# Where the relu rows of eight half-width steps are kept, and when VectorE sums them

## The chip, the core and the metric

The kernel runs on one core of a Trainium2 chip. The metric is the device time of one execution in microseconds, the median over runs. Below, PE is TensorE, DVE VectorE, ACT ScalarE, POOL GpSimd and SP SyncE; a transfer is issued from the queue of SP, ACT or POOL.

## The reference, cut to what matters

```python
e = stack([tbl_f[ids[:, f]] for f in range(32)], axis=1)      # 512 x 32 x 16, gathered rows
xk = x0 = e
for W in (W0, W1, W2):                                        # 64 outputs each
    xk = relu(einsum('bmd,bhd,mhk->bkd', x0, xk, W))
    outs.append(sum(xk, axis=2))                              # the sums that the change moves
h = concatenate([concatenate(outs, axis=1), dense_ctx], axis=1)   # 512 x 208
h = maximum(h @ W_top1 + b_top1, 0)
h = maximum(h @ W_top2 + b_top2, 0)
y = h @ W_top3                                                # 512 x 1
```

## The kernel before, in words

**Tiling.** The batch of 512 is cut into ten blocks: blocks 0 to 3 are half-width (32 examples each, 512 columns of example times dimension), blocks 4 to 9 are full-width (64 examples, 1024 columns). A step is a pair (layer, block), so there are 30 steps. A step of layer 1 or 2 multiplies 128-partition tiles of the fields with tiles of the hidden values elementwise, and PE contracts the products with the weights into a PSUM accumulator `acc`. Most products are made by DVE (line 746), in units of one to three tiles, into the buffer `vz`, which has nine places that are filled in turn; some are made by POOL (line 691) into `pz`, four places. For the five layer-0 steps of blocks 0 to 4, ACT makes the products as squares (line 810).

**Order.** The order of the steps is written out by hand (`BEGUN`, line 71), and planner functions make one program for each engine from it. `ORDER` (line 291) is the steps by the place of their last contraction: (0,0), (0,1), (1,0), (0,2), (1,1), (2,0), (0,3), (1,2), (0,4), (2,1), (1,3), and so on to (2,8), (2,9). PE's program is one list, in which a product of DVE or of POOL, once its turn has come, holds all that stands behind it.

**After the contraction of a step.** ACT writes the relu of `acc` into `relu_out` (line 858), a ring of RRING = 3 places that the steps take by their place in `ORDER`. From there the rows go three ways: by DMAs from ACT's queue into `hidden` (line 869), or through a matmul on PE (line 911, "spread"), as the next layer's factor; and DVE adds up the 16 values of each example (line 756, `dim_sums`) into `feats`. Before a relu takes a place again, ACT waits until the step that had it before is summed, spread and relayed (lines 849 to 856).

**When DVE sums.** `sum_places` (line 342) puts the sum of a step behind the first DVE unit by which at least 6 x 1024 product columns have been made since the step's own last unit, in the order of `ORDER`. `SUMS_AFTER` maps a unit's number to the sums behind it; what is left comes last (`SUMS_LAST`).

**Gathers.** POOL issues 128 indirect gathers (line 674), one for each column of `index`: 48 ahead of its first product, the others between the products as `GATHERS_IN` says. Before the first product of step (1,3) there are 13 more, before its second one more, before its third eight more. Some gathers wait for PE's progress (`PACED`) or for a spread (`BEHIND_SPREAD`). The descriptors of these gathers are written by POOL into a reserved part of each SBUF partition, whose size is an argument of the program's constructor (line 1155).

**The end.** SP copies `feats` of layers 0 and 1 into `stack01` (line 638), each after a count of `sums_done` (line 636). PE's last stage (lines 994 to 1080) needs both, and the sums of layer 2.

The units that matter below are numbered within their step from 0. (1,8) and (1,9) have five DVE units each: three tiles, three, two, two, two. (2,8) begins with a unit of three tiles.

Of the kernel before, what the change touches and what calls it, by code (L numbers as in the profile page):

```python
# [11 lines left out]
P = 128  # L12
BATCH, FIELDS, DIM, HID = 512, 32, 16, 64
CHUNK = 32
N = CHUNK * DIM
# [19 lines left out]
BLOCKS = [(pair, half * N, N, half * GATHERS // 2, GATHERS // 2) for pair in range(NARROW_PAIRS) for half in range(2)]  # L35
BLOCKS += [(pair, 0, PAIR, 0, GATHERS) for pair in range(NARROW_PAIRS, PAIRS)]
LAST = len(BLOCKS) - 1
QUARTERED = max(BLOCKS[b][0] for b in SQUARED) + 1
HALVES = [b for b, block in enumerate(BLOCKS) if block[2] == N]
# [6 lines left out]
def by_field(b):  # L46
    return int(b not in SQUARED)
# [68 lines left out]
PRING = 4  # L116
FRING = 3
RRING = 3
ORING = 2
GRING = 4  # L120
IN_FLIGHT = 3
# [52 lines left out]
def vector_program():  # L174

    program = []
    for step in BEGUN:
        mine = [(step, u) for u in range(len(vector_units(step)))]
        if step in INSIDE:
            at = next(i for i, (outer, u) in enumerate(program)  # L180
                      if outer == BEGUN[BEGUN.index(step) - 1] and u == INSIDE[step])
            program[at:at] = mine
        else:
            program += mine
    return program
# [31 lines left out]
VECTOR = vector_program()  # L217


def vectors_to(step):  # L220

    return max(i for i, (of, _) in enumerate(VECTOR) if of == step) + 1
# [68 lines left out]
ORDER = sorted(BEGUN, key=lambda step: max(i for i, (of, who, u) in enumerate(TENSOR) if of == step and who != "join"))  # L291
# [47 lines left out]
    COLUMNS.append(COLUMNS[-1] + vector_units(_step)[_u][2] * BLOCKS[_step[1]][2])  # L339


def sum_places():

    places, due = {}, list(ORDER)
    for i in range(len(VECTOR)):
        while due and vectors_to(due[0]) <= i + 1 and COLUMNS[i + 1] - COLUMNS[vectors_to(due[0])] >= 6 * PAIR:
            places.setdefault(i, []).append(due.pop(0))
    return places, due


SUMS_AFTER, SUMS_LAST = sum_places()

# [44 lines left out]
def cin_dlrm(nc, table, ids, first_row, unit, pairs, added, parts, w0a, w0b, w0c, w1, w2, wt1, bt1, wt2,  # L399
             bt2, wt3, wt1_dense, dense, out):  # L400
    with ExitStack() as ctx:
        def sb(name, shape, dt=F32):
            return ctx.enter_context(nc.sbuf_tensor(name, shape, dt))
# [4 lines left out]
        def sem(name):  # L408
            return ctx.enter_context(nc.semaphore(name))
# [12 lines left out]
        fields = [sb(f"fields_sb{s}", [P, TILES, PAIR]) for s in range(STREAMS)]  # L422
        hidden = [sb(f"hidden{s}", [P, HHALF, PAIR]) for s in range(STREAMS)]
        relu_out = [sb(f"relu_out{n}", [P, N]) for n in range(RRING)]
        vz = sb("vz", [P, VTILES, PAIR])
        pz = sb("pz", [P, PRING, PAIR])
        oz = [sb(f"oz{n}", [P, PAIR // QUART]) for n in range(ORING)]
        unit_sb = sb("unit_sb", [P, P])
# [48 lines left out]
        relu_done, sums_done = sem("relu_done"), sem("sums_done")  # L477
# [13 lines left out]
        def acc_of(step, ab):  # L491

            return acc[ab * HID:(ab + 1) * HID, ORDER.index(step) % 2, 0:BLOCKS[step[1]][2] // 2]

        def relu_of(step):
            return relu_out[ORDER.index(step) % RRING][:, 0:BLOCKS[step[1]][2] // 2]

        def hidden_of(step, g):
            _, col, cols, _, _ = BLOCKS[step[1]]
            return hidden[stream(step[1])][:, g, col:col + cols]  # L500
# [7 lines left out]
        def quarter_rows(b):  # L508

            pair, _, _, first, rows = BLOCKS[b]  # L510
            return gathered[:, pair % GRING, first:first + rows, :].rearrange("p b d -> p (b d)")
# [16 lines left out]
        def relayed_halves(step):  # L528
            return [1] if step in HALF else range(HHALF)
# [19 lines left out]
        def _(sp):  # L549
# [83 lines left out]
            sp.dma_start(wt2_sb, wt2.rearrange("(m p) n -> p m n", p=P)).then_inc(top_in, 16)  # L633
            half_cols = BATCH // 2
            for layer in range(2):
                sp.wait_ge(sums_done, ORDER.index((layer, LAST)) + 1)
                for ab in range(2):
                    sp.dma_start(stack01[layer * HID:(layer + 1) * HID, ab * half_cols:(ab + 1) * half_cols],
                                 feats[layer][ab * HID:(ab + 1) * HID, :, :].rearrange("p c j -> p (c j)")) \
                      .then_inc(stack01_in, 16)  # L640
# [7 lines left out]
        def _(pool):  # L648
            def rows_landed(i):
                pair, j = divmod(i, GATHERS)  # L650
                b, first = next((b, first) for b, (of, _, _, first, rows) in enumerate(BLOCKS)
                                if of == pair and first <= j < first + rows)
                pool.wait_ge(rows_in[b], 16 * (j - first + 1))
# [60 lines left out]
        def _(dve):  # L714
# [36 lines left out]
            def dim_sums(step):  # L751
                layer, b = step
                pair, col, cols, _, _ = BLOCKS[b]
                first, count = col // DIM // 2, cols // DIM // 2
                dve.wait_ge(relu_done, ORDER.index(step) + 1)
                nc.vector.tensor_reduce(feats[layer][:, pair, first:first + count],  # L756
                                        relu_of(step).rearrange("p (b d) -> p b d", d=DIM),
                                        op=ALU.add, axis=AX_X).then_inc(sums_done, 1)
# [21 lines left out]
        def _(act):  # L780
# [32 lines left out]
            def own_squares(step):  # L813
                b, n = step[1], OWN.index(step)
                _, _, cols, _, rows = BLOCKS[b]
                act.wait_ge(rows_in[b], 16 * rows)
                if n >= ORING:
                    act.wait_ge(oz_used, n - ORING + 1)
                nc.scalar.activation(oz[n % ORING][:, 0:cols // QUART], quarter_rows(b), ACT.Square).then_inc(oz_ready, 1)

# [8 lines left out]
            def contracted(step):  # L829
                act.wait_ge(vz_used, vectors_to(step))  # L830
                if step[0] == 0:
                    act.wait_ge(oz_used, OWN.index(step) + 1)
                if pool_units(step):
                    act.wait_ge(pz_used, pools_used_to(step))
# [8 lines left out]
            def relu(step):  # L843
                n = ORDER.index(step)
                if step in PAIRED:
                    act.wait_ge(joined, JOINED.index(step) + 1)
                else:
                    contracted(step)
                if n >= RRING:
                    layer, b = before = ORDER[n - RRING]  # L850
                    act.wait_ge(sums_done, n - RRING + 1)
                    if (layer + 1, b) in SPREAD or (layer + 1, b) in HALF:
                        act.wait_ge(factor_spread, SPREADS.index(((layer + 1, b), 0)) + 1)
                    if layer < 2 and (layer + 1, b) not in SPREAD:
                        for g in relayed_halves((layer + 1, b)):
                            act.wait_ge(relayed[(layer + 1, b), g], 32)
                half = BLOCKS[step[1]][2] // 2
                nc.scalar.activation(relu_of(step), acc[:, n % 2, 0:half], ACT.Relu).then_inc(relu_done, 1)  # L858

            def relay(step):  # L860
                _, col, cols, _, _ = BLOCKS[step[1]]
                s = stream(step[1])
                act.wait_ge(relu_done, ORDER.index(step) + 1)
                if pools_read((step[0] + 1, step[1])):
                    act.wait_ge(pz_ready, pools_read((step[0] + 1, step[1])))
                for g in relayed_halves((step[0] + 1, step[1])):
                    for ab in range(2):
                        row, at = ab * HID + g * HROWS, col + ab * cols // 2
                        act.dma_start(hidden[s][:, g, at:at + cols // 2],  # L869
                                      relu_of(step)[row:row + HROWS, None, :]  # L870
                                      .broadcast_to([HROWS, MREP, cols // 2])).then_inc(relayed[(step[0] + 1, step[1]), g], 16)
# [3 lines left out]
            for what, step, g in SCALAR:  # L875
                if what == "put":
                    put_factor(step, g)
                elif what == "squares":
                    squares(step, g)
                elif what == "own":  # L880
                    own_squares(step)
                elif what == "copy":
                    copy_hidden(step, g)
                elif what == "fold":
                    fold(step)
                else:
                    relu(step)
                    if step[0] < 2 and (step[0] + 1, step[1]) not in SPREAD:
                        relay(step)
# [12 lines left out]
        def _(pe):  # L902
# [58 lines left out]
            def contract_own(step):  # L961
# [5 lines left out]
                for q in (0, 2, 1, 3):  # L967
                    part = slice(q % 2 * quarter, (q % 2 + 1) * quarter)
                    last = nc.tensor.matmul(acc_of(step, q // 2)[:, part], w0c_sb[:, by_field(b), q, :],  # L969
                                            oz[n % ORING][:, 0:quarter], start=False, stop=q % 2 == 1)  # L970
                last.then_inc(oz_used, 1)
# [191 lines left out]
```

## Time and profile before

| what | value |
|---|---|
| runs | 333.34, 333.96, 334.33 us; median 333.96 |
| profiled execution, its own time | 333.23 us |
| its span in the trace | 331.4 us |
| granted TensorE clock, mean | 0.99 |
| PE, DVE, POOL, ACT busy | 303.6, 267.0, 244.0, 65.3 us |

The span is the stretch between the first and the last recorded instruction. The 1.8 us between it and the execution's own time lie around the program. All stretches below are in microseconds from the start of the span. "Idle before" is the time an engine did nothing before an instruction, and the name behind the arrow is what the profile holds to have ended it.

### The profile page before, as it was taken

The numbers are of one execution on the slowest core, as the hardware profiler recorded it, in microseconds if no ns is written. First come the engines' busy times: TensorE is split into PE (matmuls) and PEld (weight loads), VectorE is DVE, ScalarE is ACT, GpSimd is POOL, SyncE is SP. The second block draws the span as 40 slices with busy tenths as digits, with TensorE's granted clock in tenths as the row PEclk, the third lists the DMA queues.
The fourth block names the chain that finished last, engine by engine and source line by source line (L and its number), as shares of the span: only waits on it lengthen the run. The fifth ranks groups of instructions, "written<-read, shape, count | busy, mean of one in ns | idle before, by whom it ended". The sixth has DMA issues, their size and how long they took to land.

```text
span 331.4 us, 4576 instructions
## 1 busy us (share of the span) xinstructions
PE 303.6 (92%) x1760; PEld 131.7 (40%) x1760; DVE 267.0 (81%) x162; ACT 65.3 (20%) x105; POOL 244.0 (74%) x187
## 2 busy tenths in 40 slices
PE   0469899999869989999999899999999999999996
PEld 0335535654436233333333233344434434434334
DVE  0118399676978999999999999999899999999110
ACT  1030511435000130122122101032213032020011
POOL 5677777778888789999888799999686539966000
PEclk9997999999989999999999999999999999999999
DMA  6364848771388869687679489929979995230000
GB/s 189 95 195 138 242 107 238 206 211 21 87 267 285 292 227 297 230 269 244 203 233 318 141 251 322 323 98 266 385 316 320 313 292 130 60 85 1 0 2 0
DMA packets 32220, 65.43 MB, mean 197 GB/s; under 512 B 5702, under 2 KB 12870, under 8 KB 32198
## 3 DMA queue, kind: packets, MB, share of 16 engines
q1 hardware_dynamic: 20614, 52.28, 46.8%
q10 hardware_dynamic: 7488, 11.80, 12.3%
q0 software_dynamic: 4096, 1.06, 3.9%
q8 instruction: 14, 0.23, 0.3%
q14 instruction: 8, 0.07, 0.1%
HBM read 51.35 MB, written 1.71 MB: 160 GB/s over the span
## 4 chain that ended last, share of the span: by engine, by line
PE 63%; DVE 10%; issue 9%; POOL 4%; ACT 1%; ACTq 0%; DVEq 0%; POOLq 0%
PE acc L956 55%; DVE vz L746 9%; POOL gathered L674 3%; PE factor L1001 2%; PE factor L996 1%; POOL pz L691 1%; PE acc L969 1%; PE factor L911 1%; PE acc L951 1%; PE factor L926 1%; PE factor L1008 1%; DVE feats L756 1%; PE acc L1001 1%; ACT factor L792 0%; ACTq L869 0%
## 5 line engine op out<-in xcount | busy, mean ns | idle before, releaser
L746 DVE TENSOR_TENSOR vz<-fields_sb,factor 128x1024 f32<-128x1024 f32 (+3 forms) x113 | 229.0, 2076 | 32.2 <-PE factor L911 11.1
L956 PE MATMUL acc<-vz,w_sb 128*64 128x512 f32 (+1 forms) x1020 | 197.8, 525 | 6.4 <-DVE vz L746 6.0
L674 POOL DMA_INDIRECT gathered<-in_table,index x128 | 121.8, 952 | 38.1 <-issue 31.0
L691 POOL TENSOR_TENSOR pz<-fields_sb,hidden 128x1024 f32<-128x1024 f32 (+1 forms) x53 | 121.4, 2314 | 19.0 <-DMA hidden<-relu_out 15.0
L956 PEld LDWEIGHTS acc<-vz,w_sb 128*64 128x64 f32 x1020 | 78.6, 139 | 111.3 <-issue 84.1
L956 PE MATMUL acc<-pz,w_sb 128*64 128x512 f32 (+1 forms) x212 | 52.9, 583 | 2.7 <-POOL pz L691 2.7
L858 ACT ACTIVATE relu_out<-acc 128x512 f32<-128x512 f32 (+1 forms) x30 | 15.4, 514 | 111.2 <-PE acc L956 85.8
L792 ACT ACTIVATE factor<-hidden 128x1024 f32<-128x1024 f32 (+1 forms) x26 | 23.6, 914 | 64.5 <-DMA hidden<-relu_out 45.0
L956 PEld LDWEIGHTS acc<-pz,w_sb 128*64 128x64 f32 x212 | 17.1, 137 | 30.1 <-issue 25.7
L746 DVE TENSOR_TENSOR vz<-rotated,factor 128x2048 f32<-128x2048 f32 x10 | 22.4, 2279 | 0.0
L756 DVE TENSOR_REDUCE feats<-relu_out 128x32 f32<-128x512 f32 (+1 forms) x30 | 17.1, 570 | 6.4 <-ACT relu_out L858 6.4
L951 PE MATMUL acc<-vz,w_sb 128*64 128x512 f32 x64 | 16.4, 604 | 0.5 <-DVE vz L746 0.3
L810 ACT ACTIVATE vz<-factor 128x512 f32<-128x512 f32 (+2 forms) x24 | 12.4, 610 | 19.9 <-PE factor L926 14.3
L956 PE MATMUL acc<-vz,w_half 128*64 128x256 f32 (+1 forms) x80 | 13.5, 482 | 2.1 <-ACT vz L810 2.1
L926 PE MATMUL factor<-gathered,added_sb 32*128 32x128 f32 (+1 forms) x160 | 8.7, 344 | 3.6 <-DMA gathered<-in_table,index 3.6
L1018 PE MATMUL acc<-w_half,vz 128*128 128x64 f32 x8 | 1.9, 424 | 9.6 <-ACT w_half L874 9.6
L926 PEld LDWEIGHTS factor<-gathered,added_sb 32*128 32x128 f32 x160 | 6.5, 212 | 6.9 <-issue 6.8
L911 PE MATMUL factor<-relu_out,unit_sb 32*128 32x256 f32 (+1 forms) x56 | 8.7, 499 | 0.6 <-ACT relu_out L858 0.6
L956 PEld LDWEIGHTS acc<-vz,w_half 128*64 128x64 f32 x80 | 5.7, 152 | 8.5 <-issue 4.2
L969 PE MATMUL acc<-oz,w0c_sb 128*64 128x256 f32 (+1 forms) x80 | 9.0, 346 | 0.0
L792 ACT ACTIVATE factor<-own 128x1024 f32<-128x1024 f32 x5 | 5.1, 1027 | 18.7 <-issue 10.3
L951 PEld LDWEIGHTS acc<-vz,w_sb 128*64 128x64 f32 x64 | 4.6, 136 | 10.5 <-DVE vz L746 6.2
(35 smaller groups left out, 52.6 us busy)
## 6 DMA issues: line engine op xcount, KB each, us to landing
fields_sb<-fields SPq DMA_DIRECT2D x48, 512.0 KB, 5.0
rotated<-fields SPq DMA_DIRECT2D x20, 512.0 KB, 6.4
hidden<-relu_out ACTq DMA_DIRECT2D x38, 256.0 KB, 5.7
fields_sb<-fields SPq DMA_DIRECT2D x32, 256.0 KB, 3.3
own<-fields SPq DMA_DIRECT2D x5, 512.0 KB, 5.9
gathered<-in_table,index POOLq DMA_INDIRECT x128, 4.1
hidden<-relu_out ACTq DMA_DIRECT2D x14, 128.0 KB, 3.9
fields<-gathered SPq DMA_DIRECT2D x5, 256.0 KB, 2.2
```

The lines of the kernel that those rows point to most:

```text
L674: nc.gpsimd.indirect_dma_start(gathered[:, pair % GRING, j, :], None, table, bass.IndirectOffsetOnAxis(ap=index[:, i:i + 1], axis=0)).then ...
L691: nc.gpsimd.tensor_tensor(pz[:, at % PRING, 0:cols], fields[s][:, t, col:col + cols], hidden_of(step, g), ALU.mult).then_inc(pz_ready, 1)
L746: nc.vector.tensor_tensor(vz[:, at:at + nt, 0:cols].rearrange("p t (a n) -> p t a n", n=half), src[:, t:t + nt, col:col + cols].rearrange( ...
L756: nc.vector.tensor_reduce(feats[layer][:, pair, first:first + count], relu_of(step).rearrange("p (b d) -> p b d", d=DIM), op=ALU.add, axis ...
L792: nc.scalar.activation(factor_of(step, g), src.rearrange("p (a n) -> p a n", a=2), ACT.Copy).then_inc(factor_put, 1)
L810: last = nc.scalar.activation(made, sums, ACT.Square)
L858: nc.scalar.activation(relu_of(step), acc[:, n % 2, 0:half], ACT.Relu).then_inc(relu_done, 1)
L911: last = nc.tensor.matmul(factor_of(step, g)[:, ab, :], unit_sb[row:row + HROWS, :], relu_of(before)[row:row + HROWS, :], start=True, stop ...
L926: last = nc.tensor.matmul(added_bank(step, t, q), added_sb[row, t, :], rows[row, :], start=True, stop=True)
L951: last = nc.tensor.matmul(acc[side % 2 * HID:(side % 2 + 1) * HID, ORDER.index(step) % 2, 0:cols], weights[:, kt, :], z, start=side < 2, s ...
L956: last = nc.tensor.matmul(acc_of(step, ab), weights[:, kt, :], z[:, ab * half:(ab + 1) * half], start=start and j == 0, stop=stop and j == ...
L969: last = nc.tensor.matmul(acc_of(step, q // 2)[:, part], w0c_sb[:, by_field(b), q, :], oz[n % ORING][:, 0:quarter], start=False, stop=q % ...
```

## The change: places of their own for eight steps

The first eight half-width steps of `ORDER`, which are (0,0), (0,1), (1,0), (0,2), (1,1), (2,0), (0,3) and (1,2), get a relu place each (eight tensors of 512 columns, 2 KB of each partition). The other 22 steps share the ring of three. The sums of the eight no longer stand behind the units of the early steps; one of them stands behind each unit of DVE from unit 0 of (1,8) on, after whatever sum the old rule puts there. That gives: (0,0) behind unit 0 of (1,8), (0,1) behind unit 1, (1,0) behind unit 2, (0,2) behind unit 3, (1,1) behind unit 4; (2,0) behind unit 0 of (1,9), (0,3) behind unit 1, (1,2) behind unit 2. In the kernel before they stood behind unit 5 of (1,0); units 2, 3 and 5 of (1,1); unit 5 of (2,0); units 3 and 5 of (1,2); and unit 1 of (2,1). All other sums stay behind the units that they stood behind. The counts that ACT and SP wait for follow the new order, and the eight relus, with the three first ones of the ring, wait for no sum. The reserved part for gather descriptors becomes 8192 bytes of a partition, half of what it was.

```diff
+KEPT = 8
+KEPT_UNTIL = (1, 8)
...
+KEPT_STEPS = [step for step in ORDER if step[1] in HALVES][:KEPT]
+RINGED = [step for step in ORDER if step not in KEPT_STEPS]
 def sum_places():
-    places, due = {}, list(ORDER)
+    places, due, kept = {}, list(RINGED), list(KEPT_STEPS)
     for i in range(len(VECTOR)):
         while due and vectors_to(due[0]) <= i + 1 and COLUMNS[i + 1] - COLUMNS[vectors_to(due[0])] >= 6 * PAIR:
             places.setdefault(i, []).append(due.pop(0))
+        if kept and i >= VECTOR.index((KEPT_UNTIL, 0)):
+            places.setdefault(i, []).append(kept.pop(0))
+    assert not kept
     return places, due
...
+SUMMED = [step for i in range(len(VECTOR)) for step in SUMS_AFTER.get(i, [])] + SUMS_LAST
...
+        kept = [sb(f"kept{n}", [P, N // 2]) for n in range(KEPT)]
...
         def relu_of(step):
-            return relu_out[ORDER.index(step) % RRING][:, 0:BLOCKS[step[1]][2] // 2]
+            if step in KEPT_STEPS:
+                return kept[KEPT_STEPS.index(step)][:, :]
+            return relu_out[RINGED.index(step) % RRING][:, 0:BLOCKS[step[1]][2] // 2]
...
-                sp.wait_ge(sums_done, ORDER.index((layer, LAST)) + 1)
+                sp.wait_ge(sums_done, max(n for n, step in enumerate(SUMMED) if step[0] == layer) + 1)
...
-                if n >= RRING:
-                    layer, b = before = ORDER[n - RRING]
-                    act.wait_ge(sums_done, n - RRING + 1)
+                if step in RINGED and RINGED.index(step) >= RRING:
+                    layer, b = before = RINGED[RINGED.index(step) - RRING]
+                    act.wait_ge(sums_done, SUMMED.index(before) + 1)
...
-    nc = bacc.Bacc("TRN2", target_bir_lowering=False, num_devices=1)
+    nc = bacc.Bacc("TRN2", target_bir_lowering=False, num_devices=1, dynamic_dma_scratch_size=8192)
```

## Rows read from the trace of the kernel before

**Rows 1.** The page: each engine's busy time, and the chain that ended last.
```profile
PE 303.6 (92%) x1760; PEld 131.7 (40%) x1760; DVE 267.0 (81%) x162; ACT 65.3 (20%) x105; POOL 244.0 (74%) x187
...
PE 63%; DVE 10%; issue 9%; POOL 4%; ACT 1%; ACTq 0%; DVEq 0%; POOLq 0%
```

**Rows 2.** Busy time by stretch: PE, PEld, DVE, ACT, POOL, then clock, DMA share, GB/s.
```profile
250.00:280.00 30.00, 30.00 (x147) 12.40 (x144) 29.57 (x15) 6.93 (x10) 18.49 (x8) 1.00 0.89 273
280.00:314.00 34.00, 34.00 (x164) 13.32 (x160) 27.61 (x14) 4.82 (x6) 21.25 (x10) 1.00 0.15 35
```

**Rows 3.** Timeline of POOL around 95 us: start, length, what, idle before.
```profile
94.54 0.94 POOL L674 DMA_INDIRECT gathered<-in_table,index  x1 [0.30 <-issue]
95.50 1.28 POOL L691 TENSOR_TENSOR pz<-fields_sb,hidden 128x512 f32<-128x512 f32 x1
```

**Rows 4.** All gathers of the kernel: their time, and their time to landing.
```profile
L674 POOL DMA_INDIRECT gathered<-in_table,index x128: 940/944/1114, 3.6 to 218.8; - x128
...
  issue: 31.0, 109
...
DMA to landing us min/median/max: 2.3/4.1/6.4
```

**Rows 5.** Timeline of PE around 95 us.
```profile
96.84 0.87 PE L956 MATMUL acc<-pz,w_sb 128*64 128x256 f32 x4 [2.65 <-POOL pz L691]
97.49 7.30 PE L956 MATMUL acc<-vz,w_sb 128*64 128x256 f32 x52
```

**Rows 6.** Timeline of DVE, from the early stage.
```profile
77.56 2.35 DVE L746 TENSOR_TENSOR vz<-fields_sb,factor 128x1024 f32<-128x1024 f32 x2 [4.88 <-ACT factor L792]
79.83 0.41 DVE L756 TENSOR_REDUCE feats<-relu_out 128x16 f32<-128x256 f32 x1
80.16 5.67 DVE L746 TENSOR_TENSOR vz<-fields_sb,factor 128x1024 f32<-128x1024 f32 x4
...
100.31 2.35 DVE L746 TENSOR_TENSOR vz<-fields_sb,factor 128x1024 f32<-128x1024 f32 x2 [2.85 <-PE acc L956]
```

**Rows 7.** Busy time and granted clock (the third number from the end) around 97 us.
```profile
98.00:100.00 2.00, 2.00 (x12) 1.12 (x10) 0.00 (x0) 0.00 (x0) 1.46 (x2) 0.50 0.78 264
```

**Rows 8.** Timeline of DVE in steps (1,8), (1,9) and (2,8).
```profile
264.51 2.28 DVE L746 TENSOR_TENSOR vz<-fields_sb,factor 128x2048 f32<-128x2048 f32 x1
267.23 6.62 DVE L746 TENSOR_TENSOR vz<-fields_sb,factor 128x3072 f32<-128x3072 f32 x2 [0.43 <-PE acc L956]
...
280.95 3.35 DVE L746 TENSOR_TENSOR vz<-fields_sb,factor 128x3072 f32<-128x3072 f32 x1
```

**Rows 9.** Timeline of ACT: the factor for unit 0 of (1,9).
```profile
266.11 1.03 ACT L792 ACTIVATE factor<-hidden 128x1024 f32<-128x1024 f32 x1 [7.25 <-DMA hidden<-relu_out]
```

**Rows 10.** Timeline of PE: contractions of (1,9), the first unit of (2,8), the last stage.
```profile
270.00 4.49 PE L956 MATMUL acc<-vz,w_sb 128*64 128x512 f32 x20
...
275.15 2.77 PE L956 MATMUL acc<-vz,w_sb 128*64 128x512 f32 x12
...
283.73 4.49 PE L956 MATMUL acc<-vz,w_sb 128*64 128x512 f32 x20
...
288.88 2.77 PE L956 MATMUL acc<-vz,w_sb 128*64 128x512 f32 x12
...
313.04 1.14 PE L1042 MATMUL factor<-rotated 32*128 32x512 f32 x8
```

**Rows 11.** The chain that ended last: two places where PE runs straight behind DVE.
```profile
47.89 0.04 issue
47.94 1.94 PE acc L951 x6
...
194.30 0.14 issue
194.43 44.85 PE acc L956 x208
```

**Rows 12.** SP's transfers into `stack01`: times of issue, first and last start.
```profile
L638 SPq DMA_DIRECT2D rotated<-feats x4: 462/575/685, 268.4 to 288.7; - x4
```

## The prediction

> **What bounds the kernel now.** I first read the page: PE is busy 92% of the span, DVE 81%, POOL 74% [rows 1]. Such shares don't say which engine sets the end in the two stretches that the change touches, so I read those: the early one, which loses eight sums, and (1,8) to (1,9), which gets them.
>
> Early, the chain of waits runs through POOL. PE stands idle for 2.65 us until 96.84, and what ends it is a product of POOL, the third of step (1,3) [rows 5]. That product began at 95.50, straight behind a gather (94.54 + 0.94 = 95.48) [rows 3]. Before it stand 70 gathers, and of all 128 gathers 109 began after an "issue" gap, 31.0 us in all or 0.28 each: nothing that the profile shows holds them [rows 4]. POOL is one unbroken row of work here, so PE can't pass 96.84 whatever DVE does. DVE had run ahead as far as its places allow, and was idle for 2.85 us until PE gave one back, at 100.31 [rows 6]. Everything later starts from these two moments.
>
> Late, PE is the bound. It is busy for the whole of 250 to 280 and 280 to 314 [rows 2], and the chain stays on it from 194.43 [rows 11]. DVE works only a little ahead of it: busy 29.57 of 30 us from 250 to 280. How far ahead it is there decides what eight added sums cost.
>
> **What one sum costs DVE.** A half-width sum is busy 0.41 us, but it begins 0.08 before the product ahead of it is done, and the next product starts 0.33 after it (79.83, then 80.16) [rows 6]. So a sum pushes all later DVE work by 0.33. Eight are 2.64 us.
>
> The Trainium skill (VectorE: DVE Perf Modes, the tier table and the side-by-side of cycles) has the reduction at one element per cycle plus about 150 cycles. By that, 256 elements would take an estimated 0.42 us. It matches the busy time in the row, but not the step from start to start, and the row decides; by the page's figure the sum below would come to +1.9 us instead of +1.1.
>
> **Removed early: worth 0.** Up to (0,3), the sums' time goes into waits that stand anyway: behind them DVE is idle for 4.88 us until 77.56, for ACT's factor [rows 6]. Only the last one, (1,2) at 79.83, stands in an unbroken row of DVE work. Its 0.33 can reach PE, and then makes PE's idle time before 96.84 about 2.98 instead of 2.65. Bounds: nothing gained, or all 2.64 if POOL were not what holds PE. I take 0, since the product of POOL can't start before 95.50. Where the wait goes: DVE is idle longer until 100.31, PE longer until 96.84.
>
> **Removed waits of ACT.** A relu no longer waits for a sum three steps back. In the trace before, these sums were done long before: (1,2), the last of them, at 80.24 [rows 6], for the relu of (1,3), whose contraction ends behind 96.84. Worth 0, and what a relu could gain lies before 96.84 or in the spare time of ACT, which is busy 20% [rows 1].
>
> **Half the space for descriptors.** The trace has no row for it. From below: no gain, since all gathers take alike, 0.940 to 1.114 us [rows 4], and more gain with less space has no mechanism. From above: each time that POOL had to wait for space, it would wait for one landing, 4.1 us (at most 6.4), instead of stepping on after 0.944 + 0.28 = 1.22 [rows 4], thus 2.9 us for each wait, all of it on the path up to 95.50. I take 0: at 1.22 us a gather and 2.3 to 6.4 us to land, two to six are on the way at once, and with the full space none of 128 shows such a stall. Other places of the tensors in SBUF: 0 as well; there is no row, but the units of a form take 3.35 us wherever they lie in `vz` [rows 8].
>
> **Moved SP wait.** The copies of layer 0 into `stack01` must now wait for the sum of (0,3), at about 276 instead of 268.4; those of layer 1 go as before, the last at 288.7 [rows 12]. PE wants them at 313 [rows 10]. Their cover is over 20 us: 0.
>
> **Added late, the term that decides.** No engine waits for the sums themselves; queued behind each of them is the next product, and PE waits for that.
> 1. The sums of (0,0), (0,1), (1,0), (0,2), (1,1) stand behind units 0 to 4 of (1,8). Unit 4 ended at 264.51 + 2.28 = 266.79, so without a wait the next unit would have begun at 266.71. It began at 267.23 [rows 8], because ACT had its factor ready only at 266.11 + 1.03 = 267.14 [rows 9]. This swallows 0.52 of the 5 x 0.33 = 1.65. Unit 0 of (1,9) is late by 1.13.
> 2. It ends at 267.23 + 3.35 + 1.13 = 271.71. PE started it at 270.00 + 8 x 0.2146 = 271.72: in the row of 20 matmuls the first eight belong to unit 4 of (1,8) [rows 10]. From DVE's end to PE's start the least is 0.14 for a step's first unit and 0.04 to 0.06 for others [rows 11]. PE is 0.14 late.
> 3. With the sum of (2,0) unit 1 is 1.46 late. It ended at 267.23 + 6.62 = 273.85, now 275.31, and PE wanted it at 275.15 [rows 10]: PE 0.21 late.
> 4. Behind units 1 and 2 come (0,3) and (1,2). From unit 3 on DVE is 1.13 + 3 x 0.33 = 2.12 late. Unit 0 of (2,8) ended at 280.95 + 3.35 = 284.30 [rows 8], now 286.42, plus 0.14 is 286.56. PE started it at 283.73 + 8 x 0.2146 = 285.45 [rows 10]. PE is **1.11 us late**.
> 5. After it nothing more is lost. Unit 1 of (2,8) has the smallest lead of those behind: DVE ended it at 284.30 - 0.08 + 3.35 = 287.57 [rows 8], PE took it at 288.88 [rows 10], so 1.31, and 1.31 + 1.11 - 2.12 leaves 0.30.
>
> PE has no idle time from there to 313, and nothing to catch up with. Bounds: 0 if DVE's lead holds all of it, 2.64 if none. I take 1.11, which is worked out from the rows of just these units.
>
> **Sum.** 0 + 0 + 0 + 1.11: the profiled execution's 333.23 becomes 334.34, its span 332.5. It was 0.73 under the median, 333.96; on the median the same sum gives **335.1 us**.
>
> **The rivals.**
> - *Hidden late (no change, 334.0).* The lead of DVE before (2,8) is only 285.45 - 284.30 = 1.15 us in this one execution. If in others ACT's factor comes later than 267.14, or DVE is further ahead, the sums fill waits and cost 0 to 0.9. For it: 1.11 is a difference of numbers of that size. Against: PE has no idle time in which to hide anything. Time 334.0 to 334.9.
> - *Early gain gets through (faster, 332.4).* Releasers are inferred. If PE before 96.84 is really held by something that DVE feeds, up to 2.64 are gained, from DVE's first unit after 100.31 on, and 1.11 lost: -1.5. It decides if PE resumes before 96.8. Against: POOL's product and PE's start fit to 0.06 us (95.50 + 1.28 = 96.78).
> - *The clock (faster or slower by 1.3).* After its 2.65 us idle, PE's granted clock stood at 0.50 in 98 to 100 [rows 7], the lower level of 1.2 GHz. The 12 matmuls of the unit at 97.49 have 256 columns, half of the 512 that take 0.2146 us in [rows 10]; at the lower level each needs 0.107 more, and 12 x 0.107 = 1.3 us, and DVE's place at 100.31 hangs on them. If that low stretch falls elsewhere, 1.3 is gained: 333.8 with the late loss. If the longer idle time, 2.98, draws it out, it costs up to 1.3 more: 336.4. The Trainium skill (TensorE: Matmul & The Clock Gate, Part 1) has idle time as what drops the clock; the trace agrees, and by that rule a longer idle time speaks against the change.
> - *No cover late (slower, 336.6).* All eight sums reach PE, +2.64, if the 0.52 wait before (1,9) moves along with DVE and the lead is gone.
> - *POOL waits for descriptor space (slower, 336.8 and up).* One wait before 95.50, +2.9, on top of which DVE still pays late.
>
> **How the numbers follow.** A measurement of this kernel can tell about 0.3%, 1.0 us, from no change. Chances: forecast, 334.6 to 335.6, 0.45; hidden late 0.25; early gain gets through 0.08; clock 0.10, half each way; no cover 0.08; descriptor space 0.04. The forecast sits at the edge of 1.0 us (334.96), so I give it 0.30 to slower and 0.15 to same. Slower: 0.30 + 0.05 + 0.08 + 0.04 = 0.47. Same: 0.15 + 0.25 + 0.03 = 0.43. Faster: 0.10, from the early gain and a little of the clock. The range, 333.2 to 336.6, holds the forecast, the hidden case with the spread of the runs, and the full price of eight sums; it leaves out the early gain and the descriptor stall.
>
> **What would show it.** Right: PE resumes at 96.8 again, its idle time before it is about 3.0 us, DVE restarts at 100.3, gathers step on by about 1.22; DVE has eight reductions of 0.41 between 255 and 278; (2,8)'s first contraction starts with a wait for DVE of about 0.9, and a small one stands before units 0 and 1 of (1,9). Wrong: PE resumes earlier than 96.8; a gap over 1 us between gathers; no idle time of PE between 270 and 290; or a loss that lies before 250.

## The result, and the profile after

| | before | after |
|---|---|---|
| median, 16 runs each | 333.43 us (332.68 to 334.45) | 334.64 us (333.89 to 335.98) |
| profiled execution, its span | 333.23, 331.4 us | 334.53, 332.7 us |

The ratio is 1.0034, 95% interval [1.0022, 1.0046]: the changed kernel is slower by 0.34%, 1.1 us (0.7 to 1.5 by the interval). The prediction had +1.11. Its 335.1 us came out 0.5 above the measured 334.64, because it was built on a median of three runs, 333.96; sixteen runs gave 333.43.

Of the changed kernel, the page's busy times and the head of its chain, and then the stretches of [rows 2] and [rows 7]:
```profile
PE 302.9 (91%) x1760; PEld 125.2 (38%) x1760; DVE 267.1 (80%) x162; ACT 65.2 (20%) x105; POOL 244.6 (74%) x187
...
PE 62%; DVE 12%; DMA 11%; issue 9%; POOL 2%; ACT 2%; SPq 1%; ACTq 1%; DVEq 0%
```
```profile
96.00:98.00 2.00, 1.61 (x8) 1.01 (x10) 0.17 (x1) 0.00 (x0) 1.54 (x3) 0.50 0.82 214
...
250.00:280.00 30.00, 29.33 (x142) 10.06 (x140) 29.36 (x21) 6.13 (x8) 17.76 (x8) 1.00 0.88 263
280.00:314.00 34.00, 33.33 (x158) 12.65 (x154) 29.68 (x14) 4.28 (x5) 22.08 (x10) 1.00 0.16 39
```
The busy times hardly moved. What moved is where PE is idle: before it was busy for all of 250 to 314, now 0.67 us are missing in each of the two stretches. DVE's instructions from 250 to 280 are 21 instead of 15.

The early place, in the timelines of POOL, PE and DVE of the changed kernel:
```profile
95.06 1.28 POOL L705 TENSOR_TENSOR pz<-fields_sb,hidden 128x512 f32<-128x512 f32 x1
...
96.39 1.12 PE L970 MATMUL acc<-pz,w_sb 128*64 128x256 f32 x4 [3.49 <-POOL pz L705]
...
99.81 2.35 DVE L760 TENSOR_TENSOR vz<-fields_sb,factor 128x1024 f32<-128x1024 f32 x2 [3.64 <-PE acc L970]
```
PE again begins 0.05 us behind the end of POOL's product (95.06 + 1.28 = 96.34), as it did before [rows 3, 5]. The eight sums are gone from before this point, and all that came of it is more idle time: PE's grew from 2.65 to 3.49 us, DVE's from 2.85 [rows 6] to 3.64.

The late place, in DVE's timeline, the same stretch as [rows 8]:
```profile
255.13 0.68 DVE L770 TENSOR_REDUCE feats<-relu_out 128x32 f32<-128x512 f32 x1
255.72 0.41 DVE L770 TENSOR_REDUCE feats<-kept 128x16 f32<-128x256 f32 x1
256.05 3.35 DVE L760 TENSOR_TENSOR vz<-fields_sb,factor 128x3072 f32<-128x3072 f32 x1
...
267.48 0.41 DVE L770 TENSOR_REDUCE feats<-kept 128x16 f32<-128x256 f32 x1
268.53 3.35 DVE L760 TENSOR_TENSOR vz<-fields_sb,factor 128x3072 f32<-128x3072 f32 x1 [0.64 <-issue]
271.80 0.41 DVE L770 TENSOR_REDUCE feats<-kept 128x16 f32<-128x256 f32 x1
...
278.51 0.41 DVE L770 TENSOR_REDUCE feats<-kept 128x16 f32<-128x256 f32 x1
278.84 11.00 DVE L760 TENSOR_TENSOR vz<-fields_sb,factor 128x2048 f32<-128x2048 f32 x4
```
Each sum takes its 0.41 and puts the next instruction off by 0.33 (255.72 to 256.05, 278.51 to 278.84). And PE's timeline, as [rows 10], with ACT's factor, as [rows 9]:
```profile
269.48 1.89 PE L970 MATMUL acc<-vz,w_sb 128*64 128x512 f32 x8
272.03 2.79 PE L970 MATMUL acc<-vz,w_sb 128*64 128x512 f32 x12 [0.67 <-DVE vz L760]
...
275.53 2.80 PE L970 MATMUL acc<-vz,w_sb 128*64 128x512 f32 x12
...
286.72 2.79 PE L970 MATMUL acc<-vz,w_sb 128*64 128x512 f32 x12 [0.67 <-ACT relu_out L872]
...
267.41 1.03 ACT L806 ACTIVATE factor<-hidden 128x1024 f32<-128x1024 f32 x1 [9.08 <-DMA hidden<-relu_out]
```
The two idle times of PE stand where steps 2 and 4 of the sum put them: ahead of unit 0 of (1,9) and of unit 0 of (2,8). Their sizes are not those of the sum, by which PE loses 0.14 at the first and 1.11 - 0.21 = 0.90 at the second; the part on the prediction says why. The name behind the second arrow misleads. The unit's product ended at 286.57 and PE began 0.15 later, as far behind as at unit 0 of (1,9) (271.88 to 272.03); the relu named there, that of (1,9), only ended at the same time. In the kernel before, PE began this unit at 285.45, ahead of that relu, so it doesn't wait for it.

### The profile page after: what moved, and what is told of

Its sections match the earlier page's. It is cut to its first block, busy times and chain, and to the rows that moved or that the text cites. A ratio compares the mean times of both kernels' runs of the same rounds, so it can differ in the third digit from the quotient of the medians.

```text
span 332.7 us, 4566 instructions
## 1 busy us (share of the span) xinstructions
PE 302.9 (91%) x1760; PEld 125.2 (38%) x1760; DVE 267.1 (80%) x162; ACT 65.2 (20%) x105; POOL 244.6 (74%) x187
## 3 DMA queue, kind: packets, MB, share of 16 engines
q0 software_dynamic: 4096, 1.06, 3.9%
## 4 chain that ended last, share of the span: by engine, by line
PE 62%; DVE 12%; DMA 11%; issue 9%; POOL 2%; ACT 2%; SPq 1%; ACTq 1%; DVEq 0%
PE acc L970 53%; DVE vz L760 12%; DMA rotated<-fields 4%; DMA fields_sb<-fields 3%; PE factor L940 3%; POOL gathered L688 2%; DMA hidden<-relu_out 2%; PE factor L1015 2%; PE factor L1010 1%; PE acc L983 1%; PE factor L925 1%; ACT vz L824 1%; PE factor L1022 1%; DMA gathered<-in_table,index 1%; PE acc L965 1%
## 5 line engine op out<-in xcount | busy, mean ns | idle before, releaser
L970 PEld LDWEIGHTS acc<-vz,w_sb 128*64 128x64 f32 x1020 | 74.1, 139 | 116.6 <-issue 87.4
L872 ACT ACTIVATE relu_out<-acc 128x512 f32<-128x512 f32 (+1 forms) x22 | 12.3, 559 | 103.7 <-PE acc L970 82.5
L970 PEld LDWEIGHTS acc<-pz,w_sb 128*64 128x64 f32 x212 | 15.8, 138 | 32.5 <-issue 26.1
L770 DVE TENSOR_REDUCE feats<-relu_out 128x32 f32<-128x512 f32 (+1 forms) x22 | 13.9, 631 | 5.4 <-ACT relu_out L872 5.4
L965 PEld LDWEIGHTS acc<-vz,w_sb 128*64 128x64 f32 x64 | 4.6, 136 | 10.5 <-DVE vz L760 6.2
L983 PEld LDWEIGHTS acc<-oz,w0c_sb 128*64 128x64 f32 x80 | 5.6, 137 | 4.9 <-issue 3.6
```

Source lines behind the costliest of these rows:

```text
L965: last = nc.tensor.matmul(acc[side % 2 * HID:(side % 2 + 1) * HID, ORDER.index(step) % 2, 0:cols], weights[:, kt, :], z, start=side < 2, s ...
L970: last = nc.tensor.matmul(acc_of(step, ab), weights[:, kt, :], z[:, ab * half:(ab + 1) * half], start=start and j == 0, stop=stop and j == ...
```

## The experiments

Eleven kernels were run. Ratios are to runs of the kernel before on the same chip, five rounds each. Three chips were used, so medians of different rows don't compare, only ratios do.

| run | median, us | ratio [95%] |
|---|---|---|
| space for descriptors alone | 332.86 | 0.9992 [0.9980, 1.0005] |
| eight sums left out | 333.36 | 1.0007 [0.9995, 1.0019] |
| eight sums made twice | 334.27 | 1.0033 [1.0019, 1.0047] |
| sums in DVE's wait at 97 | 333.37 | 1.0010 [0.9998, 1.0023] |
| sums from (2,8) on | 333.74 | 1.0016 [1.0003, 1.0029] |
| six gathers later | 333.45 | 1.0010 [0.9991, 1.0029] |
| thirteen gathers later | 332.72 | 0.9994 [0.9979, 1.0009] |
| and a tile of (2,6) to DVE | 332.33 | 0.9981 [0.9966, 0.9996] |
| before, weights later | 333.76 | 1.0014 [1.0002, 1.0027] |
| changed, weights later | 334.51 | 1.0041 [1.0026, 1.0056] |
| thirteen gathers, tile, weights later | 332.12 | 0.9971 [0.9943, 0.9999] |

### The space for descriptors alone

```diff
-    nc = bacc.Bacc("TRN2", target_bir_lowering=False, num_devices=1)
+    nc = bacc.Bacc("TRN2", target_bir_lowering=False, num_devices=1, dynamic_dma_scratch_size=8192)
```


> The kernel before with nothing changed but the reserved part for gather descriptors, 8192 bytes instead of the full size. Theory: 0 (within 0.3 us of the kernel before), each gather 0.94 us busy and POOL's third product of (1,3) at 95.5 as before. Rival (POOL waits for space): each wait adds about 2.9 us, so +1.1 or more with a gap of over 1 us somewhere between gathers.

0.9992, and the interval takes in 1. All gathers of this run, from its source view:
```profile
L674 POOL DMA_INDIRECT gathered<-in_table,index x128: 940/944/1109, 3.6 to 218.5; - x128
...
  issue: 30.4, 106
```
No gather is longer than with the full space (1109 ns against 1114 in [rows 4]), and the waits named "issue" are 0.29 each, against 0.28. POOL shows no wait for space. The rival falls.

This kernel is the kernel before in all else, so its trace also tells how much one execution of that kernel differs from another. ACT's factor for (1,9) started 8.3 us after its relay began (258.57 to 266.84) instead of 7.2, and DVE waited for it. DVE's unit 0 of (1,9), and PE at the last unit of (1,8) and at unit 1 of (2,8):
```profile
267.96 3.35 DVE L746 TENSOR_TENSOR vz<-fields_sb,factor 128x3072 f32<-128x3072 f32 x1 [1.49 <-issue]
...
269.68 4.58 PE L956 MATMUL acc<-vz,w_sb 128*64 128x512 f32 x20
...
289.11 2.77 PE L956 MATMUL acc<-vz,w_sb 128*64 128x512 f32 x12
```
PE went from 0.32 ahead of the trace before (269.68 to 270.00) to 0.23 behind it (289.11 to 288.88). A late factor costs 0.55 us here without any moved sum.

### The eight sums left out: the early half alone

```diff
 def sum_places():
...
+    places = {i: [step for step in of if step not in LEFT_OUT] for i, of in places.items()}
     return places, due
```
`LEFT_OUT` is the eight steps. Their sums are not computed at all.

> The kernel before without the sums of the eight half-width steps (they are left out altogether; DVE sets feats to zero in its idle first 8 us instead, and the counts follow). This is the early half of the change alone. Theory (POOL holds PE at 96.8): 0, at most 0.3 us gained; PE's idle time before 96.8 grows from 2.65 to about 3 us. Rival (the early gain gets through): -1.0 to -2.6 us. Rival (the clock): the longer idle time of PE moves the stretch of low granted clock, +0.5 to +1.3 us or as much less.

1.0007 [0.9995, 1.0019]: taking 2.64 us of work from DVE ahead of 97 gives nothing. PE in this run:
```profile
96.82 0.65 PE L964 MATMUL acc<-pz,w_sb 128*64 128x256 f32 x4 [3.17 <-POOL pz L696]
```
It resumes at 96.82, where it did before (96.84), and has been idle for 3.17 us instead of 2.65. The rival in which the early gain gets through is excluded: 1.0 us would have been 0.9970.

One execution makes the same test the other way round. In the profiled one of "changed, weights later" (below), DVE and PE were late in the early stage: DVE came out of its wait for ACT's factor at 79.82 instead of 77.56.
```profile
79.82 7.94 DVE L761 TENSOR_TENSOR vz<-fields_sb,factor 128x1024 f32<-128x1024 f32 x6 [5.13 <-ACT factor L807]
...
96.54 0.65 PE L971 MATMUL acc<-pz,w_sb 128*64 128x256 f32 x4 [0.42 <-POOL pz L706]
```
PE took POOL's product as soon as it was there (95.19 + 1.30 = 96.49) and was not late behind it: only its idle time shrank, from 2.65 to 0.42 us.

### The eight sums made twice: the late half alone

```diff
-    places, due, kept = {}, list(RINGED), list(KEPT_STEPS)
+    places, due = {}, list(ORDER)
...
+    kept = list(KEPT_STEPS)
+    for i in range(VECTOR.index((KEPT_UNTIL, 0)), len(VECTOR)):
+        if kept:
+            places.setdefault(i, []).append(kept.pop(0))
```


> The changed kernel, but each of the eight sums is made at both places: where the kernel before has it, and again behind the units of (1,8) and (1,9). This is the late half alone, with the early work kept. Theory: as slow as the changed kernel, +1.1 us (0.9 to 1.8) on the kernel before, all of it between 267 and 286 us. Rival (the early gain gets through, and hides part of a late cost of 2.6): +1.7 to +2.6, clearly slower than the changed kernel.

1.0033 [1.0019, 1.0047], against 1.0034 for the change itself: the late half is the whole cost, as far as the intervals can tell. In this execution ACT's factor for (1,9) came at 266.28 + 1.03 = 267.31, close to the 267.14 of the sum. PE:
```profile
270.07 4.63 PE L971 MATMUL acc<-vz,w_sb 128*64 128x512 f32 x20
...
275.41 2.80 PE L971 MATMUL acc<-vz,w_sb 128*64 128x512 f32 x12
...
286.61 2.79 PE L971 MATMUL acc<-vz,w_sb 128*64 128x512 f32 x12 [0.67 <-ACT relu_out L873]
```
At the last unit of (1,8) PE was 0.07 behind the trace before (270.07 to 270.00). At unit 1 of (1,9) it was 0.26 behind, at unit 0 of (2,8) 286.61 - 285.45 = 1.16. Less the 0.07, the sums cost 0.19 and 1.09 at these two places, where the prediction had 0.21 and 1.11.

### The sums in a place where DVE waits

```diff
-KEPT_UNTIL = (1, 8)
+KEPT_UNTIL = ((2, 2), 1)
...
-        if kept and i >= VECTOR.index((KEPT_UNTIL, 0)):
+        while kept and i >= VECTOR.index(KEPT_UNTIL):
```


> The changed kernel with the eight sums behind unit 1 of (2,2), where DVE in the kernel before is idle for 2.85 us until 100.3 (and 3.6 us in the changed one): 8 x 0.33 = 2.64 us fit in. Neither the early places nor the late ones carry them. Theory (early sums are worth nothing, late sums are the whole cost): 0, within 0.3 us of the kernel before, and 1.1 us faster than the changed one. Rival (the new places of the tensors, the shorter waits of ACT or the descriptor space have a part in the cost): it stays 0.5 to 1.1 us slower than before.

```profile
96.40 2.70 DVE L770 TENSOR_REDUCE feats<-kept 128x16 f32<-128x256 f32 x8
100.14 2.35 DVE L760 TENSOR_TENSOR vz<-fields_sb,factor 128x1024 f32<-128x1024 f32 x2 [1.03 <-PE acc L970]
```
All eight sums lie one behind the other in DVE's wait, and the wait is still not full: 1.03 us are left of it. The ratio is 1.0010 [0.9998, 1.0023], not told apart from 1, and its trace runs level with that of the kernel before from 100 to the end (PE's unit 0 of (2,8) starts 0.19 earlier, as does everything from 250 on; POOL's product of (1,3) started 0.23 earlier in this execution, at 95.27). The new places, ACT's shorter waits and the descriptor space, which this kernel has as well, have no part in the cost that could be seen.

### The sums from (2,8) on: how much lead there is

```diff
-KEPT_UNTIL = (1, 8)
+KEPT_UNTIL = (2, 8)
...
-    places, due, kept = {}, list(RINGED), list(KEPT_STEPS)
+    places, due, kept = {}, list(RINGED), sorted(KEPT_STEPS, key=lambda step: step[0] == 2)
```


> The changed kernel with the eight sums behind the units of (2,8) and (2,9), from unit 0 of (2,8) on, the one of (2,0) last. In the trace before, DVE's leads over PE at the units that follow are 1.32, 1.97, 3.00, 2.31, 2.47, 3.12, 3.50 and 4.08 us, and the sums take 0.33, 0.66, 0.99, 1.32, 1.65, 1.98, 2.31 and 2.64 off them: none falls under 0.8. Theory (a late sum costs only where DVE's lead is used up): 0, within 0.3 us, although as many sums stand in the stretch in which PE is busy throughout. Rival (DVE work added after 250 costs its time wherever it stands, or the later copies into stack01 hold PE's last stage): +0.7 to +2.6 us.

1.0016 [1.0003, 1.0029], between the two: about half the cost, not none. The trace says why. Its PE is 1.56 us late at the last contraction (313.62 to 312.06), but 1.34 of that came ahead of the first moved sum. PE was 0.70 late already at the last unit of (1,8) (270.70 to 270.00), and 0.64 came with the factor of (1,9):
```profile
268.41 1.03 ACT L806 ACTIVATE factor<-hidden 128x1024 f32<-128x1024 f32 x1 [8.84 <-DMA hidden<-relu_out]
...
269.53 6.62 DVE L760 TENSOR_TENSOR vz<-fields_sb,factor 128x3072 f32<-128x3072 f32 x2 [2.03 <-issue]
...
273.03 2.80 PE L970 MATMUL acc<-vz,w_sb 128*64 128x512 f32 x12 [0.41 <-DVE vz L760]
```
ACT's factor for (1,9) came 2.30 us later than in [rows 9]. DVE waited for it for 2.03 us, and its lead over PE at unit 0 of (2,8) was 0.19 instead of 1.15. With that little left, sums do cost: the other 0.22 by the end. The lead that the expectation took from one execution isn't the same in all of them. That is the part of the theory that this run corrects; that a sum costs only what the lead doesn't hold stands.

### Loading the last weights later: two runs on the late factor

SP's loads of the top layers' weights wait for ACT's second factor of (1,9), in the kernel before and in the changed one:
```diff
             sp.wait_ge(vz_ready, vector_made(vectors_to((0, LAST - 1))))
+            sp.wait_ge(factor_put, PUT.index(((1, LAST), 1)) + 1)
             sp.dma_start(wt1_sb, wt1[0:2 * HID, :]).then_inc(top_in, 16)
```


> The kernel before, but SP issues the top layers' weights and the dense rows (1.3 MB, issued between 261.6 and 268 so far) only when ACT has made the factor for (1,9)'s second half, near 272. In nine executions of different kernels ACT started the factor of (1,9)'s first unit 7.0 to 9.1 us after the relay of (0,9) began, while the DMA engines were full; where it took over 8, PE waited for DVE there. Theory (these loads are what the relay competes with): 6.5 us or less, no wait of PE at (1,9), and 0 to -0.4 us on the kernel before. Rival: the spread has another cause, the start stays 7 to 9 us after, and the time is that of the kernel before.

> The changed kernel with the same later loads. With an early factor DVE comes to (1,9) held only by the five sums, so unit 0 begins where the sums let it and the loss by the end is the 1.11 us of the sum in the prediction, without what a late factor adds. Theory: +0.8 to +1.1 us on the kernel before, 1.0 to 1.1 on the kernel before with the later loads, and 0 to 0.4 faster than the changed kernel. Rival (the sums' cost is mostly that of the late factor): at most 0.4 us over the kernel before.

The theory of the first falls. ACT started the factor 6.9 us after the relay began in the one run (259.81 to 266.71) and 8.0 in the other, and the kernel before became slower, 1.0014 [1.0002, 1.0027]. In its trace the next relay is the slow one: the factor started 8.1 us after it began (273.49 to 281.56), against 4.9 in the trace before, and DVE waited for it:
```profile
282.69 3.35 DVE L747 TENSOR_TENSOR vz<-fields_sb,factor 128x3072 f32<-128x3072 f32 x1 [1.06 <-ACT factor L793]
```
This wait cost PE nothing in this execution, however: PE was 0.91 behind the trace before at the last unit of (1,8) (270.91 to 270.00) and 0.92 at the last stage (313.96 to 313.04). Where the median lost its 0.14% isn't shown, and what makes the factor of (1,9) vary between executions stays open.

The second run still tells what it was made for. It stands 1.0041/1.0014 = 1.0027 over its own counterpart, 0.9 us (0.3 to 1.6, an estimate from the two intervals); its factor was ready at 266.45 + 1.03 = 267.48, while the sums kept DVE busy beyond that, so nothing of the loss is the factor's:
```profile
269.56 3.76 PE L971 MATMUL acc<-vz,w_sb 128*64 128x512 f32 x16
...
286.07 2.79 PE L971 MATMUL acc<-vz,w_sb 128*64 128x512 f32 x12 [0.67 <-ACT relu_out L873]
```
PE went from 0.44 ahead of the trace before (269.56 to 270.00) to 0.62 behind (286.07 to 285.45): 1.06 us by the sums.

### Six gathers later: is it POOL?

```diff
-GATHERS_IN = {(1, 3): (13, 1, 8), (1, 4): (8, 6, 5, 3), (1, 5): (3, 0, 1, 1), ...
+GATHERS_IN = {(1, 3): (13, 1, 2), (1, 4): (14, 6, 5, 3), (1, 5): (3, 0, 1, 1), ...
```


> The kernel before, with six of the eight gathers ahead of POOL's third product of (1,3) put behind it, ahead of the first product of (1,4); the sums stay. POOL's work up to the first product of (1,4) is the same in sum. Theory (this product holds PE until 96.8): it now starts near 88.0, PE's 2.65 us idle time and the low clock behind it go, DVE's wait of 2.85 us until 100.3 goes too, and the kernel is faster by 2 to 3 us. Rival (PE is held by something else, or what follows is held by POOL or the DMAs): less than 0.5 us gained.

The mechanism was right and the time was wrong: 1.0010 [0.9991, 1.0029], nothing gained. PE and the clock of this run around 95:
```profile
94.53 0.65 PE L956 MATMUL acc<-pz,w_sb 128*64 128x256 f32 x4
95.01 3.19 PE L956 MATMUL acc<-vz,w_sb 128*64 128x256 f32 x28
...
98.00:100.00 2.00, 2.00 (x18) 0.95 (x16) 2.00 (x2) 0.00 (x0) 1.52 (x2) 1.00 0.63 250
```
The idle time of 2.65 us is gone, and so is the low granted clock that followed it (1.00 in 98 to 100, against 0.50 in [rows 7]), and PE and DVE ran 3.06 us ahead of the trace before up to 130. So POOL's third product of (1,3) was what held them. But the gain went again, at POOL's later products:
```profile
140.16 1.08 PE L956 MATMUL acc<-pz,w_sb 128*64 128x512 f32 x4 [0.30 <-POOL pz L691]
...
149.57 1.08 PE L956 MATMUL acc<-pz,w_sb 128*64 128x512 f32 x4 [0.61 <-POOL pz L691]
...
202.76 1.08 PE L956 MATMUL acc<-pz,w_sb 128*64 128x512 f32 x4 [0.37 <-POOL pz L691]
205.07 1.08 PE L956 MATMUL acc<-pz,w_sb 128*64 128x512 f32 x4 [1.23 <-POOL pz L691]
```
In the kernel before, POOL's last product of (1,6) ends its row of three at 197.40 + 7.02 = 204.42, and PE took it at 204.76, by these rows of the kernel before (POOL, then PE, whose last four of twelve matmuls are that product's, 203.04 + 8 x 0.2146 = 204.76):
```profile
197.40 7.02 POOL L691 TENSOR_TENSOR pz<-fields_sb,hidden 128x1024 f32<-128x1024 f32 x3
...
203.04 2.77 PE L956 MATMUL acc<-pz,w_sb 128*64 128x512 f32 x12
```
That is 0.34 us of lead, of which 0.06 is needed (with the gathers later, 198.00 + 7.01 = 205.01 to 205.07): whatever PE gains ahead of 204, no more than 0.28 of it can pass unless POOL is earlier too. In the profiled execution POOL was 0.6 later than in the trace before (198.00 to 197.40), so not even that passed. This second place of the kind was missing in the prediction.

### Thirteen gathers later, and a tile less for POOL

```diff
-    4, (1, 5): 4, (2, 4): 4, (2, 5): 1, (1, 6): 5, (1, 7): 4, (2, 6): 5, (2, 7): 6, ...
+    4, (1, 5): 4, (2, 4): 4, (2, 5): 1, (1, 6): 5, (1, 7): 4, (2, 6): 4, (2, 7): 6, ...
...
+GATHERS_IN = {(1, 3): (13, 1, 2), (1, 4): (14, 6, 5, 3), (1, 5): (1, 0, 0, 0), (2, 4): (6, 1, 0, 0), (2, 5):
+    (9,), (1, 6): (4, 7, 0, 0, 0), (1, 7): (4, 1, 0, 0), (2, 6): (3, 0, 0, 0)}
```
The first kernel has the gathers alone (with five entries for (2,6)), the second both.

> The kernel before, with six gathers behind the third product of (1,3) as in the run with six gathers later, four more moved from between the products of (1,5) ahead of the first of (2,4), and three from (1,6) to (1,7). In the run with six later PE gained 3.06 us up to 130 and gave it back where it waited for POOL's products of (1,5) at 140 to 149 (1.35 us) and of (1,6) at 202 to 205 (2.1 us). Theory (POOL, which works without a break up to 232, is the bound behind all of these places): the gain now holds until the next product that has no lead, the fifth of (2,6), which had 0.75 us: -0.3 to -0.7 us. Rival (DMA or DVE takes it): 0.

> As the run with thirteen gathers moved, and one tile of step (2,6) made by DVE instead of POOL (four by POOL, four by DVE in two units). That takes 2.35 us from POOL ahead of the fifth product of (2,6), which goes, and adds 1.1 us to DVE, which had waits of 0.67 and 0.83 us around (2,6). Theory (POOL bounds up to 232): -0.7 to -2 us. Rival (DVE has too little lead behind (2,6), or the DMAs of the fields come late): not faster than the run without it, or slower than before.

With the gathers alone, 0.9994 [0.9979, 1.0009], not told apart from the kernel before. The trace ran 4.07 us ahead at 165 and 2.7 ahead at 212, and of these 2.7 it lost all but 0.7 where it was said, at the fifth product of (2,6):
```profile
231.48 1.08 PE L956 MATMUL acc<-pz,w_sb 128*64 128x512 f32 x4 [1.24 <-POOL pz L691]
```
With a tile of (2,6) taken from POOL too, 0.9981 [0.9966, 0.9996], just short of what was expected (0.7 to 2 us): 0.6 us faster than the kernel before, and 1.7 us faster than the changed one. Its page has POOL 3.2 us less busy than the page after (2.6 less than the page before), and the span is 329.6:
```profile
PE 303.3 (92%) x1760; PEld 124.9 (38%) x1760; DVE 268.3 (81%) x163; ACT 65.2 (20%) x105; POOL 241.4 (73%) x186
```
With the weights later as well it was 0.9971 [0.9943, 0.9999]; that the two add is not shown, as the intervals overlap.

> The run with thirteen gathers moved and a tile of (2,6) given to DVE, with the same later loads. It was at 0.9981 of the kernel before. Theory: the two add, 0.9965 to 0.9980. Rival: with the relay no longer the limit at (1,9), POOL's first product there or DVE's lead is, and nothing is added.

## Why the prediction was right, point by point

- **POOL holds PE at 96.84.** Right, and shown from both sides: taking DVE work away ahead of it gave 1.0007, taking POOL work away let PE pass. The prediction read 96.84 as a fixed time, which it is not. POOL's third product of (1,3) began anywhere from 95.06 to 96.21 in the nine profiled kernels that have the gathers in the old order. In eight of them PE reached the last unit of (1,8) 174.4 to 174.5 us later, whatever the sums, the idle times and the clock had been (174.9 in "before, weights later"). POOL's row is unbroken from a gather at 23.8 to 25.1 us on, ahead of which it waits up to 1.4 us, by the profile for a spread on PE; the product follows 71.1 to 71.3 us later. So up to 1.15 us of what two single executions differ by can come from there; in the changed kernel's, POOL was 0.44 earlier (95.06 to 95.50).
- **What one sum costs, 0.33.** Right, in the seven of eight places of the changed kernel where no wait follows the sum (0.32 or 0.33). The estimate of 0.42 us by the Trainium skill (VectorE: DVE Perf Modes, the tier table and the side-by-side of cycles) fits the busy time of 0.41, but the sum that it gives, +1.9, doesn't fit the 1.09 and 1.06 of the two traces without a late factor.
- **Removed early: 0.** Right in time. A reading was wrong: the sums up to (0,3) don't all go into waits that stand anyway. The sum of (2,0), at 67.49, stands on the chain of the kernel before:
```profile
67.49 0.35 DVE feats L756
67.84 1.64 issue
69.48 1.76 DVE vz L746
71.23 0.04 issue
71.28 2.54 PE acc L956 x20
```
With the sums left out, DVE came out of its wait for ACT's factor at 77.34 instead of 77.56, and PE's idle time grew by 0.52, not by the 0.33 of the sum of (1,2). In the changed kernel it grew by 0.84, with an execution that ran ahead from the start (DVE's first product at 22.94 instead of 23.65) and POOL 0.44 earlier. It made no difference, as the wait took it all.
- **ACT's waits, other places, descriptor space, the SP wait: 0.** Right; the first two are covered by the run with the sums in DVE's wait, the third by its own. The copies into `stack01` began at 276.4 (the sum said 276) and still ended ahead of need.
- **Added late: 1.11.** Right as a mechanism, and met within 0.05 us where no late factor of (1,9) interfered: 1.09 and 1.06. That the median of 16 runs came so close too (+1.1, interval 0.7 to 1.5) is in part luck, as the factor is not always on time. In the profiled execution of the changed kernel the term came out larger: PE went from 0.52 ahead of the trace before (269.48 to 270.00) to 1.27 behind (286.72 to 285.45), 1.79 in all. There the factor was ready at 268.44 instead of 267.14, and DVE, held by five sums already, waited for it 0.72 from start to start (267.48 + 0.33 = 267.81 to 268.53). Step 1 of the sum has 5 x 0.33 - 0.52 = 1.13; with this wait it is 1.85. The span grew by only 1.3 because that execution was 0.5 ahead earlier, with POOL. A late factor costs the kernel before as well, 0.55 in the run with the descriptor space alone; by these two executions the sums cost 1.79 - 0.55 = 1.24 with a late factor, an estimate, as the two factors were not equally late. How often it is late in the 16 runs isn't seen, as one was profiled.
- **"Late, PE is the bound", from 194.43.** Incomplete. PE takes POOL's product at 204.76 with 0.28 us to spare, so POOL, which has no break up to 231, is a bound beside it. The prediction didn't need this, since its early gain was 0 anyway; it would have been wrong for any change that does gain early, as the run with six gathers later shows.
- **The rivals.** The early gain and the descriptor space are excluded. The clock: the low stretch came earlier in the changed kernel (0.50 already in 96 to 98) but was not longer, as the granted clock over 90 to 106 was 0.89 in both kernels; and the execution that had none of it ("changed, weights later", 1.00 there) was only 0.44 us ahead at 270, with its POOL 0.31 ahead. "Hidden late" was half right as a mechanism: DVE's lead at unit 0 of (2,8), 1.15 us in the trace before, was anything from under 0.2 to 1.4 in the other profiled kernels without added sums ahead of it. But in the one profiled execution of the changed kernel the late factor hid nothing of the sums: they cost more, not less. "No cover late" is excluded by the interval, whose upper end is 1.5 us against 2.64.

## What to carry to other kernels

Work that is moved off an engine before a point where another engine's unbroken row of work holds everything is worth nothing, and the profile shows such a point as an idle time that grows or shrinks with what lies ahead of it; look for the next such point too, by the lead of each of the holding engine's results over their use. Work moved into a stretch where the bounding engine has no idle time costs what the lead of its supplier doesn't hold, and that could be added up unit by unit from one trace to within 0.05 us for executions like it. The lead itself is a number of one execution: look at several before resting on it. Eight small sums were free in a wait of DVE that stood in the trace at 97, and cost 1.1 us 160 us later.

## What was not expected of the hardware

- Half the space for descriptors changed nothing that could be seen in 128 gathers, most of which follow each other by 1.25 us (0.9992 [0.9980, 1.0005]).
- ACT's factor of (1,9) started 6.9 to 9.1 us after its relay began, over thirteen profiled executions. In the two executions that differ only by the descriptor space it was 7.2 and 8.3 us, and DVE's lead over PE at unit 0 of (2,8) 1.15 and under 0.2. Taking 1.3 MB of other loads out of the way didn't shorten it reliably (6.9, 8.0 and 8.6 us in three runs).
- After an idle time of 2.65 and of 3.49 us, PE's granted clock fell to 1.2 GHz for a stretch (0.50 in 98 to 100 of [rows 7], and in 96 to 98 after the change). All eight profiled executions with 2.4 to 3.5 us of idle time there have a mean of 0.89 from 90 to 106. The five others, four kernels with the gathers moved and "changed, weights later" with 0.42 us, stayed at 2.4 GHz (1.00).
